# A fused transformer block on one NeuronCore: where the value row and the third head's q and k stand in the order of two engines

## The reference

```
ada = cond @ ada_w + ada_b                    # shift1, scale1, gate1, shift2, scale2, gate2
x1  = ln(x) * (1 + scale1) + shift1
q, k, v = split(x1 @ qkv_w + qkv_b)           # 16 heads of 128
att = softmax(q @ k.T / sqrt(128)) @ v        # within each sequence of 32
x   = x + gate1 * (att @ out_w + out_b)
x2  = ln(x) * (1 + scale2) + shift2
x   = x + gate2 * (gelu(x2 @ ffn_w1 + b1) @ ffn_w2 + b2)
# ternary network: activations rounded to 8 bits, weights to -1, 0 or 1 times a factor
h   = silu(bit(x, w1, g1)) * bit(x, w2, g2)
out = input + bit(h, w3, g3)
```

## Time and profile before

| | us |
|---|---|
| median of 3 runs | 321.92 (321.91 to 322.14) |
| the profiled execution | 322.68 |
| its span, first to last instruction | 320.5 |
| PE busy | 310.7 (97%) |
| DVE busy | 224.0 (70%) |
| ACT busy | 183.3 (57%) |
| POOL busy | 124.8 (39%) |

### The profile page before, as it was taken

How to read it: one execution, slowest core, us unless ns; L and a number is a source line. 1 busy time by engine, 2 the same in 40 slices (tenths; PEclk the granted TensorE clock), 3 DMA queues, 4 the chain that set the end, 5 groups by cost and what they waited for, 6 DMA issues and landing times.

```text
span 320.5 us, 9863 instructions
## 1 busy us (share of the span) xinstructions
PE 310.7 (97%) x4197; PEld 276.9 (86%) x4197; DVE 224.0 (70%) x448; ACT 183.3 (57%) x356; POOL 124.8 (39%) x109
## 2 busy tenths in 40 slices
PE   8999999999999999999999999999999999999986
PEld 7879989899998989888898997779998879998665
DVE  4747985955995985606568139879368688995996
ACT  2747383555435474556433926587536677468793
POOL 2338304100940893565420522146430244315591
PEclk9999999999999999999999999999999999999999
DMA  7991990410039343120020000200020200200011
GB/s 232 299 357 58 285 338 7 141 27 2 2 98 233 106 130 133 36 66 2 5 66 4 0 18 17 69 2 2 2 68 0 68 4 2 68 0 2 0 35 65
DMA packets 21026, 24.41 MB, mean 76 GB/s; under 512 B 1972, under 2 KB 18520, under 8 KB 20984
## 3 DMA queue, kind: packets, MB, share of 16 engines
q1 hardware_dynamic: 20608, 23.50, 24.2%
q10 hardware_dynamic: 376, 0.30, 0.3%
HBM read 22.68 MB, written 1.11 MB: 74 GB/s over the span
## 4 chain that ended last, share of the span: by engine, by line
PE 80%; DVE 7%; ACT 5%; issue 4%; DMA 2%; SPq 1%; POOL 0%; ACTq 0%; DVEq 0%
PE proj_banks L580 34%; PE out_bank L580 17%; PE wide_banks L580 5%; PE proj_banks L643 4%; PE turn_bank L580 4%; PE att_banks L673 3%; PE wide_banks L865 3%; DMA stage<-in_L_cond_qkv_w 2%; PE att_banks L580 2%; PE wide_banks L673 1%; ACT work L1898 1%; PE att_banks L865 1%; PE wide_banks L748 1%; PE proj_banks L865 1%; ACT L1757 1%
## 5 line engine op out<-in xcount | busy, mean ns | idle before, releaser
L1764 ACT ACTIVATE q_t<-proj_banks,bias_cols 128x256 f32<-128x256 f32 x64 | 30.3, 474 | 48.3 <-PE proj_banks L580 48.0
L580 PE MATMUL proj_banks<-x_hi,w_hi 128*128 128x256 f32 x252 | 53.2, 292 | 0.6 <-ACT k_t L1764 0.5
L580 PE MATMUL proj_banks<-x_lo,w_hi 128*128 128x256 f32 x252 | 49.8, 279 | 0.0
L580 PE MATMUL proj_banks<-x_hi,w_lo 128*128 128x256 f32 x252 | 49.7, 279 | 0.0
L580 PEld LDWEIGHTS proj_banks<-x_hi,w_hi 128*128 128x128 f32 x252 | 38.7, 189 | 4.5 <-issue 1.8
L580 PEld LDWEIGHTS proj_banks<-x_lo,w_hi 128*128 128x128 f32 x252 | 38.5, 189 | 0.0
L580 PEld LDWEIGHTS proj_banks<-x_hi,w_lo 128*128 128x128 f32 x252 | 38.3, 188 | 0.0
L1260 DVE TENSOR_TENSOR v_sb<-proj_banks,bv_row 128x512 f32<-128x512 f32 x32 | 21.7, 683 | 23.0 <-PE proj_banks L580 13.7
L1764 ACT ACTIVATE k_t<-proj_banks,bias_cols 128x256 f32<-128x256 f32 x64 | 30.0, 468 | 0.0
L580 PE MATMUL out_bank<-wo_hi,at_hi 128*128 128x256 f32 x128 | 21.6, 291 | 0.5
L2108 POOL TENSOR_TENSOR w_lo<-stage,w_hi 128x1024 fp32r<-128x1024 f32 x6 | 14.3, 2392 | 19.9 <-DVE w_hi L1215 14.2
(11 more groups left out here) (327 smaller groups left out, 780.7 us busy)
## 6 DMA issues: line engine op xcount, KB each, us to landing
stage<-in_L_cond_qkv_w SPq DMA_DIRECT2D x16, 256.0 KB, 4.7
gate<-gate_rows_scratch SPq DMA_DIRECT2D x48, 64.0 KB, 2.5
stage<-in_L_cond_qkv_w SPq DMA_DIRECT2D x4, 512.0 KB, 6.0
stage<-in_L_cond_out_w SPq DMA_DIRECT2D x16, 128.0 KB, 3.6
work<-in_L_ffn_w SPq DMA_DIRECT2D x2, 1024.0 KB, 9.4
xin<-in_x SPq DMA_DIRECT2D x7, 256.0 KB, 3.8
bv_row<-in_L_cond_qkv_b SPq DMA_DIRECT2D x4, 256.0 KB, 5.7
work<-in_L_cond_ada_w SPq DMA_DIRECT2D x1, 1024.0 KB, 10.0
```

What stands on the lines that cost most here:

```text
L580: mm = pe.matmul(dst, l, r, start=start and i == 0, stop=stop and i == len(seq) - 1)
L1764: act.activation(dst[:, h, :], proj_bank[h % 2][:, s * QT:(s + 1) * QT], ACT.Identity, bias=bias_cols[:, c:c + 1]).then_inc(qk_kept, 1)
```

## The change

Two steps are moved, and nothing is added or removed. In units 3, 5 and 6 DVE keeps value row 0 before it turns the attended rows of the unit before, where it did so after both turns. In units 13 and 15 ACT keeps q and k of head 2 before the exponential of unit u - 1, where it did so after it.

```diff
--- before.py
+++ after.py
@@ -1292,9 +1292,12 @@
 
             def attention_tail(u):
                 if u > 0:
+                    if u in TERN_UNITS:
+                        keep_v(u, 0)
                     for p in range(2):
                         at_turn(u - 1, p)
-                    keep_v(u, 0)
+                    if u not in TERN_UNITS:
+                        keep_v(u, 0)
                     for p in range(2):
                         at_low(u - 1, p)
                     if u == 6:
@@ -1982,8 +1985,9 @@
                 if a >= 0:
                     silu(a, 1, 1)
                     load_table(ACT.Exp)
+                keep_qk(u, 2)
+                if a >= 0:
                     exponent(u - 1)
-                keep_qk(u, 2)
                 keep_qk(u, 3)
                 if a >= 0:
                     square_hidden(a, 0)
```

## The result

| | before | after |
|---|---|---|
| median, 4 runs each | 322.03 (321.91 to 322.65) | 326.24 (325.98 to 326.36) |
| the profiled execution | 322.68 | 326.31 |
| its span | 320.5 | 324.1 |

The changed kernel is slower: ratio 1.0121 [1.0091, 1.0152]. A ratio here is taken over the executions in the chip's usual fast state, with its 95% interval in brackets, and is not exactly the quotient of the medians. The forecast was 324.4 with a range up to 325.7, so the direction is right and the measured time lies above the range. Two more comparisons of the same code gave 1.0079 [1.0059, 1.0099] and 1.0086 [1.0061, 1.0110], medians 2.81 and 2.49 us above before (forecast: 2.46).

The account below looks back on a forecast made before the run. PE's instruction list was taken as the bound, busy 310.7 of 320.5 us. Terms 0.24 + 0.16 + 1.36 + 0.70 = 2.46 added to 321.92 gave 324.4 us, 8-in-10 range 323.1 to 325.7.

Parts of the forecast that it names:

- Units 3 and 5, +0.24 and +0.16: Later turns make the second high part late, so `out_proj` starts 0.24 us later in unit 3, 0.16 in unit 5.
- Unit 6, +1.36: Late turns delay the first weight cast and the group behind it, so PE starts `qk_unit(7, 0)` 1.36 us later.
- unit 6 has hidden room: Rival: PE's start at 108.92 was set by the transposes before it, so 1.36 falls away: 323.0 us; 5%.
- the blocked cast: Unit 6's second weight cast on DVE, 2.52 us beside POOL's low part, as far behind the first cast as before.
- Units 13 and 15, +0.35 each: Exponential 0.72 us later makes the value row and `out_proj` 0.35 late; `v_unit`'s 0.23 gain is waited away there.
- DVE's unbroken row: Units 13 and 15: DVE work from row sum to second norm's add, then a 0.28 gap, too short for 0.72.
- The lock: Rival, units 13 and 15: POOL's power starts first, delaying the second norm's add 0.65 us; 1.3 in all, 325.7; 15%.
- The edit keeps its gain: Rival, units 13 and 15: `out_proj(12, 0)` did not wait for high parts; gain of 0.46 stands, 323.2 us; 12%.
- faster: Rival: turns may be late for free; `score` wins 0.6, `v_unit` 0.46, unit 6 loses nothing: 320.9 us; 5%.
- nothing: Rival: nothing measurable, the terms cancel, as with unit 6 at 0 and half of the others; 3%.
- The range: 8 in 10, from the kept gain to the lock: 323.1 to 325.7 us; the forecast's own range 323.8 to 324.9.

Follow-up runs that it names:

- both repeats: The changed kernel with both edits, timed twice more against before: 325.18 against 322.37 us, ratio 1.0079, and 324.66 against 322.17, ratio 1.0086.
- before again: The unchanged kernel timed against itself for a second trace, no edit: 322.76 against 322.60 us, ratio 1.0003.
- units 3 and 5 alone: Value row 0 kept before the turns in units 3 and 5 only, against before: 323.18 against 322.60 us, ratio 1.0016.
- the second cast alone moved: Against before, only unit 6's second cast of weights moved behind the subtraction of the row maximum: 322.27 against 322.37 us, ratio 1.0000.

## Why the prediction was right and where it was wrong

- *Units 3 and 5, +0.24 and +0.16.* Held, by the step named: `out_proj` has become the late one and stands 0.14 behind the second high part. Measured +0.25 to +0.32 and +0.15 to +0.19 over four traces. The sizes are right against the very trace that they were read from, and that is partly luck: it is late at both places, and against a usual trace of before they are about +0.4 and +0.35.
- *Unit 6, +1.36.* Held: +1.36 in all four traces that have this edit alone or with the rest. The rival that unit 6 has hidden room falls. What was missing in my account is that the blocked cast is one carrier of the delay, the ratio instructions are a second, ready behind it, and the last cast of weights in unit 7 is a third.
- *Units 13 and 15, +0.35 each.* Held: +0.39 and +0.34 with ACT's edit alone, +0.33 to +0.40 in the traces of both edits, but for +0.66 in unit 13 of the first. That the path goes through DVE's unbroken row was tested by shortening the row: the price went in unit 15 and fell in unit 13. One detail was misplaced: what `v_unit` wins is waited away at `attend(12)` already, which starts when it did before, and not at `out_proj`.
- *The lock.* Falls. It was to come if POOL's power began first; POOL began at 216.76 and DVE's add at 216.83, and the add took 0.69; so it did in both units of both repeats, with POOL 0.03 to 0.07 ahead. By the prediction's rule for this rival the delay was certain once POOL was first, and the rule does not hold for this pair; starts on POOL are rough in a profile, but all six lie the same way. POOL's mean took 0.19 where it took 0.34 beside the add.
- *The edit keeps its gain; faster; nothing.* All fall with the two repeats, whose intervals begin at 1.0059.
- *The range.* This is the step that failed: the sum has terms for the five changed places alone. Whatever unchanged code does from execution to execution stands in it at nothing, and 0.2% (0.64 us) was taken for all that a measurement can be off, so the upper bound of 325.7 is the lock and no more. The measured 326.24 is 1.84 above the forecast; 0.11 of this is that before measured 322.03 and not 321.92. The first comparison has 4.21 us between its medians. In the pair of traces 2.75 of it stands at the five changed places (0.30 of this is the stop inside `score`), and 1.00 in the first 55 us, where both kernels are the same; -0.13 is spread over the rest, which makes the 3.62 at 300 us. The remaining 0.59 is that the trace of before is itself 0.65 above its median and that of after 0.07 above its own. So what the sum left out (1.46) is larger than what it mis-sized (0.29, the stop inside `score`). That the profiled execution of before stood 0.76 above the median of runs that agreed within 0.23 was in front of me and said that executions differ by more than the three showed. The 12 later executions lie between 324.0 and 325.7, with the forecast of 324.4 inside.

What stays open: why all four first executions of the changed kernel lie above all twelve later ones. The opening's 0.67 and the stop in `score` are seen in one of the four only; the other three have no trace. The three later comparisons ran on three chips, and the record does not name the chip of the first; whether it matters was not tested.

## What to carry to other kernels

A take-out moved ahead of other work wins at most the wait of the one that needs it, and it makes all that it overtakes late by its own length plus its own wait; put filler ahead of an instruction that isn't ready, not behind it. Before a step is moved on an engine, follow its row to the next idle gap: a delay shorter than that gap dies there, a longer one comes out behind it, less the gap (here 0.72 less 0.37, the value row's 214.18 less 213.21 + 0.60, came out as 0.33 to 0.40 in seven of the eight places measured). And when a sum of local terms is near a microsecond, read it from the shifts of single instructions, ask for the spread of many executions, and let the range hold that spread too.

## What the runs showed of the hardware

- *The opening differs from execution to execution.* At 20 us PE stands between -0.74 and +2.89 us against the trace of before in the 13 other traces, though no instruction before unit 3 was changed in any. In some the cast of the first weights on ACT waits longer for its DMA: 0.43 us before, 1.09 after, 1.53 in the kernel with +2.89. In others it is the cast of x, which waits for DVE: 0.42 before, 1.64 in before again (+0.69), 2.38 in units 3 and 5 alone (+1.37). ACT's row after:

```profile
11.74 1.05 ACT L1793 CAST w_hi<-stage 128x1024 fp32r<-128x1024 f32 x1 [1.09 <-DMA stage<-in_L_cond_qkv_w]
```

- *The granted clock fell once behind an idle stretch of PE.* After 1.91 us idle in the opening it went from 1.00 to 0.50 (1.2 GHz) for some 3.5 us, which cost 1.62 (the second cast alone moved). The executions of before at 325.3 to 326.3 have the same low mean clock, 0.994 or 0.995; they have no trace.
- *PE stops for issue alone.* Inside `score`'s 64 small matmuls there are stops of up to 0.6 us put down to issue, three in the trace after (1.5 us in all), and not the same number in all traces.
- *A POOL instruction of 1024 columns holds up the smallest DVE instruction*: 2.18 us for 128x3, against 0.15 for one of the same shape that ran (109.19) before POOL began. A reciprocal of that shape was not held up (0.18 at 109.38). A POOL power of one column that began 0.07 ahead (216.76) did not hold up a DVE add of 512 (0.69).
